# Attention preparation spread over two iterations, and the first two MLP groups prepared in the last batches

## The chip, the cores and the metric

The kernel runs on one core of a Trainium2 chip. The metric is the device time of one execution in microseconds.

## The reference

One transformer block with conditioning, for x of 8 batches x 256 tokens x 144 channels (16 heads of 9):

```
sh1, sc1, g1, sh2, sc2, g2 = split(swish(c) @ w_mod + b_mod, 6)
xn  = ln(x) * (1 + sc1) + sh1
q, k, v = heads(xn @ w_qkv + b_qkv)
q = ln(q) * g_q ; k = ln(k) * g_k            # over the 9 channels of a head
o = softmax(q k^T / 3) v
x = x + g1 * (o @ w_proj + b_proj)
xn2 = ln(x) * (1 + sc2) + sh2
x = x + g2 * (gelu(xn2 @ w1 + b1) @ w2 + b2)  # hidden width 576
```

## The kernel before

A batch n has its 256 tokens in two tiles of 128 partitions (I = 2). Each of the five engines has a queue written out by hand, with semaphores between them; an engine runs its queue strictly in order, so a wait holds all that stands behind it. The order within an iteration is that of the function `iteration` of each engine's block.

**Attention of batch n** is cut into 8 units u. TensorE makes `scores(n, u)` (L1088, four matmuls into two of the four banks of `ps_s`), ScalarE takes the exponential (`exponentials`, L552), and TensorE multiplies with v (`values(n, u)`, L1103, eight matmuls into `ps_o[:, 1]`). `scores(n, u)` waits for exponential u - 2, `values(n, u)` for exponential u. After units 3 and 7 ScalarE copies the sums out (`output`, L559).

**Preparation of batch b** runs beside the attention of the batches before it, in these steps: GpSimd standardises and modulates x (`standardise` L354, `modulate` L372 and L376); VectorE splits it in a high and a low f16 part (`stack`, L712, L715); TensorE transposes (`transpose_x`, L1015), VectorE copies out (`xT_out`, L721); TensorE multiplies (`make_qkv`, L1022); ScalarE squares (`squares`, L516) and copies the raw q, k, v (`raw_out`, L523); VectorE sums (`sums`, L726); ScalarE takes the roots by Ln and Exp (`roots`, L528, L532); VectorE refines them in three Newton steps (L1276 to L1280) and scales k and q (`norm_qk`, L738); GpSimd multiplies q with the gains (`gains`, L383, L389) and places v (`v_slots`, L397); VectorE splits k and q (`split_k` L750, L753; `split_q` L760, L763; the second instruction of each is the low part, `klo` and `qlo`); TensorE transposes (`transpose_k`, `transpose_q`, L1029) and VectorE copies out (`k_out` L770, `q_out` L777).

**Output of batch n**: TensorE transposes the sums (`transpose_o`, L1113), VectorE divides (`normalise`, L836, L838), TensorE transposes by token (`transpose_o_tok`, L1122), VectorE copies (`channels`, L844), TensorE projects (`project`, L1131), VectorE gates and adds and takes statistics (`projected` L849, `residual` L855, L858).

In iteration n of before, the x of n+2 goes up to qkv, the q and k of n+1 are made, and of n-1 the output is transposed, divided and copied; its projection is in n+1.

**MLP**: four groups k of two batches (T = 4 tiles). VectorE aggregates the statistics (`aggregate`, L928) and standardises (`standardise2`, L901), GpSimd modulates (`modulate2`, L464, L468), VectorE splits (`stack2`, L912, L915), TensorE transposes (`transpose_z`, L1197), VectorE copies out (`zT_out`, L922), TensorE makes 5 hidden tiles of a group (`hidden`, L1209), ScalarE takes gelu (L609), TensorE multiplies with w2 (`mlp_out`, L1226), VectorE finishes (`final`, L943, L949). The weights w1 are split by one GpSimd instruction (L446) and one of VectorE (L964). Before, all of group 0 to 2 gets its roots at once, after the residual of batch 5, and `transpose_z(0)` stands in TensorE's queue behind the last batch's seventh unit.

Of the kernel before, what the change touches and what calls it, by code (L numbers as in the profile page):

```python
# [90 lines left out]
def build(nc, x, cT, w_mod, b_mod, w_qkv, g_q, g_k, w_proj, b_proj, w1, w2, b2, ident, lo_rows, out):  # L91
    with ExitStack() as ctx:
# [80 lines left out]
        T = 2 * I  # L173
        EARLY = (NB - 1) * T
# [96 lines left out]
        def proj_bank(n):  # L271

            return ps_o[:, 0, :] if n < B - 2 else ps_x[:, 1, :]

# [57 lines left out]
        def _(pool):  # L332
# [105 lines left out]
            for it in range(1, 2):  # L438
                iteration(it * 2, 0)
                iteration(it * 2 + 1, 1)  # L440
            iteration(B - 4, 0)
            iteration(B - 3, 1, norms=False)
            iteration(B - 2, 0, norms=False)
# [38 lines left out]
        def _(act):  # L482
# [79 lines left out]
            def early_roots():  # L562

                act.wait_ge(stat2, EARLY)
                nc.scalar.activation(ly2[:, 0:EARLY], mv2[:, 0:EARLY, 1], ACT.Ln, bias=eps[:, 0:1]).then_inc(root_act.sem, 1)
                act.wait_ge(root_act.sem, root_act.after(0, "ln"))
                nc.scalar.activation(y2[:, 0:EARLY], ly2[:, 0:EARLY], ACT.Exp, scale=-0.5).then_inc(root_act.sem, 1)

            def iteration(n, par, first=False, makes=True, ahead=True):
# [21 lines left out]
                exponentials(n, 6)  # L591
# [3 lines left out]
            for it in range((B - 4) // 2):  # L595
                iteration(it * 2 + 1, 1)
# [5 lines left out]
            output(B - 1, 1, 1)  # L602
# [11 lines left out]
        def _(dve):  # L614
# [245 lines left out]
            def iteration(n, par, first=False, makes=True, ahead=True):  # L860

                if ahead and not first:
                    stack(n + 2, prep)
                if makes:
                    sums(n + 1, prep)
                if ahead and first:
                    stack(n + 2, prep)
                if n >= 2:
                    projected(n - 2)
                if makes:  # L870
                    norm_qk(n + 1, prep)
                if not first:
                    normalise(n - 1)
                if makes:
                    split_k(n + 1, prep)
                if not first:
                    channels(n - 1)
# [6 lines left out]
                if n >= 2:  # L884
                    residual(n - 2)
# [447 lines left out]
```

## Time and profile before

| | us |
|---|---|
| median of 3 runs (lowest, highest) | 204.68 (202.39, 205.91) |
| the profiled execution | 202.29 |
| its span in the trace | 200.5 |
| TensorE busy | 166.0 (83%) |
| VectorE busy | 125.7 (63%) |
| ScalarE busy | 108.9 (54%) |
| GpSimd busy | 65.5 (33%) |

The span is the time from the first to the last instruction of the trace. A busy time is the union of the engine's instructions; two that follow each other on an engine overlap a little, so the time that one takes in a queue (start to next start) is a little less than its duration. "Clock" is the share of TensorE's full clock that was granted: 1.00 is 2.4 GHz, 0.50 is 1.2 GHz.

### The profile page before, as it was taken

What the parts mean: (1) busy time and instruction counts of PE and PEld (TensorE: products, weight loads), DVE (VectorE), ACT (ScalarE), POOL (GpSimd) and SP (SyncE); (2) the same over time, 40 slices, a digit from 0 to 9 for tenths busy, and PEclk for the clock granted to TensorE, in tenths of its full rate; (3) what the DMA queues carried; (4) which work ended last, traced back from release to release, by engine and by line L of the source; (5) the groups of instructions that cost most, each with busy time, mean ns of one, the idle gap of its engine ahead of it and who ended that gap; (6) DMA issues with size and microseconds to landing.
All of it is one profiled execution on the core that took longest, in us unless ns stands there. A gap on an engine that the chain in (4) does not pass through costs nothing.

```text
span 200.5 us, 3873 instructions
## 1 busy us (share of the span) xinstructions
PE 166.0 (83%) x1504; PEld 93.9 (47%) x1504; DVE 125.7 (63%) x312; ACT 108.9 (54%) x146; POOL 65.5 (33%) x81
## 2 busy tenths in 40 slices
PE   0009982749979999999999999899659999999983
PEld 0005131413434454544644545344316796979773
DVE  3269568819548587679677774955856786564212
ACT  2001024255998879978888799976842404132320
POOL 8103513067418146173290201600462352220000
PEclk9999999999999999999999999999856999999999
DMA  0993028950000000000000000000000000101101
GB/s 10 247 211 120 5 51 251 399 158 0 3 2 0 3 3 0 0 3 0 3 0 5 0 3 2 0 3 0 3 0 0 0 3 0 60 3 59 59 0 59
DMA packets 4535, 8.67 MB, mean 43 GB/s; under 512 B 821, under 2 KB 3071, under 8 KB 4406
## 3 DMA queue, kind: packets, MB, share of 16 engines
q1 hardware_dynamic: 4228, 8.41, 14.0%
q8 instruction: 12, 0.20, 0.4%
q14 instruction: 7, 0.06, 0.1%
q10 hardware_dynamic: 288, 0.01, 0.1%
HBM read 7.21 MB, written 1.21 MB: 42 GB/s over the span
## 4 chain that ended last, share of the span: by engine, by line
PE 73%; DVE 9%; DMA 6%; ACT 3%; POOL 3%; issue 3%; SPq 1%; POOLq 0%; ACTq 0%
PE ps_o L1103 15%; PE ps_o L1226 10%; PE ps_s L1209 9%; PE ps_s L1088 8%; PE ps_x L1022 8%; DMA pTs<-in_b_mod 6%; PE ps_x L1029 4%; PE ps_o L1131 4%; PE ps_x L1113 4%; PE ps_s L1006 3%; PE ps_o L1015 3%; PE ps_x L1197 2%; PE ps_s L1000 2%; POOL z2s L464 2%; DVE kst L753 2%
## 5 line engine op out<-in xcount | busy, mean ns | idle before, releaser
L552 ACT ACTIVATE pTs<-ps_s,escale 128x1024 f32<-128x1024 f32 x64 | 68.9, 1109 | 17.1 <-PE ps_s L1088 16.1
L1103 PE MATMUL ps_o<-pTs,v 128*32 128x256 f32 x512 | 42.9, 410 | 5.0 <-ACT raw L523 2.5
L609 ACT ACTIVATE late<-ps_s 120x512 f32<-120x512 f32 (+1 forms) x20 | 11.9, 596 | 26.1 <-PE ps_s L1209 26.1
L1088 PE MATMUL ps_s<-qT,kT 32*128 32x256 f16 x256 | 24.3, 282 | 1.0 <-DVE qT L777 1.0
L1226 PE MATMUL ps_o<-w_sb,late 120*128 120x144 f32 (+1 forms) x160 | 20.7, 287 | 0.7 <-ACT late L609 0.7
L1226 PEld LDWEIGHTS ps_o<-w_sb,late 120*128 120x128 f32 (+1 forms) x160 | 19.9, 190 | 1.2 <-ACT late L609 1.2
L1209 PE MATMUL ps_s<-late,w1s 110*120 110x512 f16 (+1 forms) x80 | 18.8, 386 | 0.0
L1103 PEld LDWEIGHTS ps_o<-pTs,v 128*32 128x32 f32 x512 | 10.5, 110 | 17.5 <-ACT pTs L552 7.1
L1088 PEld LDWEIGHTS ps_s<-qT,kT 32*128 32x128 f16 x256 | 7.1, 93 | 24.4 <-issue 20.8
L464 POOL TENSOR_TENSOR z2s<-z2s,mbc 128x576 f32<-128x576 f32 x4 | 8.4, 2092 | 28.7 <-DVE z2s L901 28.7
L397 POOL COPY v<-raw 128x288 f32<-128x288 f32 x8 | 4.0, 496 | 41.8 <-DVE ssum L726 34.9
L1000 PE MATMUL ps_s<-pTs,c_s 73*128 73x288 f32 (+1 forms) x8 | 4.2, 707 | 15.1 <-DMA pTs<-in_b_mod 15.1
L1022 PE MATMUL ps_x<-wq,xT 110*128 110x432 f16 x64 | 15.9, 401 | 0.8 <-DVE xT L721 0.8
L354 POOL TENSOR_SCALAR z<-xall,mv,rstd 128x144 f32<-128x144 f32 x14 | 13.2, 951 | 10.2 <-DVE rstd L1280 5.2
L726 DVE TENSOR_REDUCE ssum<-sq 128x64 f32<-128x576 f32 x8 | 6.0, 752 | 13.8 <-ACT sq L516 13.8
L1209 PEld LDWEIGHTS ps_s<-late,w1s 110*120 110x120 f16 (+1 forms) x80 | 10.5, 134 | 6.8 <-issue 1.2
L559 ACT ACTIVATE oT<-ps_o 128x512 f32<-128x512 f32 x16 | 9.6, 599 | 3.9 <-PE ps_o L1103 3.9
L389 POOL TENSOR_TENSOR qg<-qn,gbc 128x288 f32<-128x288 f32 x8 | 6.7, 832 | 14.7 <-DVE qn L738 14.7
L943 DVE TENSOR_TENSOR late<-ps_o,mbc 128x288 f32<-128x288 f32 x8 | 3.6, 454 | 11.5 <-PE ps_o L1226 11.5
L1022 PEld LDWEIGHTS ps_x<-wq,xT 110*128 110x128 f16 x64 | 6.3, 108 | 9.4 <-issue 5.4
L1000 PEld LDWEIGHTS ps_s<-pTs,c_s 73*128 73x128 f32 (+1 forms) x8 | 2.5, 330 | 16.0 <-DMA pTs<-in_b_mod 15.1
L1113 PE MATMUL ps_x<-id,oT 128*128 128x128 f32 x64 | 8.7, 278 | 1.2 <-ACT oT L559 1.2
(115 smaller groups left out, 263.4 us busy)
## 6 DMA issues: line engine op xcount, KB each, us to landing
mbc<-mod_rows SPq DMA_DIRECT2D x6, 432.0 KB, 7.4
late<-in_w SPq DMA_DIRECT2D x1, 990.0 KB
xall<-in_x SPq DMA_DIRECT2D x1, 864.0 KB, 13.6
out<-late SPq DMA_DIRECT2D x3, 288.0 KB, 2.3
z2s<-in_w_qkv SPq DMA_DIRECT2D x1, 742.5 KB
mbc<-mod_rows SPq DMA_DIRECT2D x2, 288.0 KB, 6.4
pTs<-in_w_mod SPq DMA_DIRECT2D x1, 486.0 KB
w_sb<-in_w SPq DMA_DIRECT2D x1, 337.5 KB
```

Source lines behind the costliest of these rows:

```text
L354: nc.gpsimd.tensor_scalar(z[:, i, :], xall[:, b, i * H:(i + 1) * H], mv[:, t, 0:1], rstd[:, t:t + 1], ALU.subtract, ALU.mult).then_inc(S.m ...
L464: nc.gpsimd.tensor_tensor(by_batch(z2a), by_batch(z2), m2(k, A2), ALU.mult).then_inc(ln2_mod.sem, 1)
L552: nc.scalar.activation(pT[u % NP].rearrange("p g n -> p (g n)"), ps_s[:, 2 * (u % 2):2 * (u % 2) + 2, :].rearrange("p a n -> p (a n)"), AC ...
L559: nc.scalar.activation(oT[par][:, 2 * pair:2 * pair + 2, :].rearrange("p j n -> p (j n)"), ps_o[:, 1, :], ACT.Copy).then_inc(o_out, 1)
L609: nc.scalar.activation(hT[k % 2][0:FW[f], f, :], ps_s[0:FW[f], (NF * k + f) % 4, :], ACT.Gelu_apprx_tanh, scale=UNSCALE).then_inc(gelued, 1)
L1000: mm = nc.tensor.matmul(ps_s[:, 2 + b, 0:2 * H], c_s[0:k, h, b:b + 1].broadcast_to([k, P]), wm_sb[0:k, h, 0:2 * H], start=(h == 0), stop=( ...
L1022: mm = nc.tensor.matmul(ps_x[:, i, 0:QKV], xT[:, c, i * P:(i + 1) * P], wq[:, c, :], start=(c == 0), stop=(c == NC - 1))
L1088: mm = nc.tensor.matmul(ps_s[:, 2 * (u % 2) + a, half * N:(half + 1) * N], kT[par][rows, j, i * P:(i + 1) * P], qT[par][rows, j, :], start ...
L1103: mm = nc.tensor.matmul(ps_o[SLOT * g:SLOT * (g + 1), 1, (j % 2) * N:(j % 2 + 1) * N], v[par][:, i, h, :], pT[u % NP][:, g, :], start=(i = ...
L1113: tr = nc.tensor.transpose(ot[:, i, j // 2, j % 2], oT[par][:, j, i * P:(i + 1) * P], id32[:])
L1209: mm = nc.tensor.matmul(ps_s[0:FW[f], m % 4, :], w1s[:, c, f * FT:f * FT + FW[f]], zT[k % 2][:, c, :], start=(c == 0), stop=(c == NC - 1))
L1226: mm = nc.tensor.matmul(ps_o[:, n, i * H:(i + 1) * H], hT[k % 2][0:r, f, t * P:(t + 1) * P], w2_sb[0:r, f, :], start=(f == 0), stop=(f == ...
```

## The change

- The preparation of a batch is spread over two iterations: in iteration n the qkv, squares, raw copy, sums and roots are those of n+2 (x of n+3 is stacked and transposed, x of n+4 standardised), while norms, splits and transposes of q and k are those of n+1, made right at the start of the iteration.
- The output is later: `transpose_o` of n-1 stands near the end of iteration n, `normalise(n - 1)` is VectorE's last step of the iteration, and the transpose by token, `channels`, projection and residual of n-1 follow in iteration n+1 (there as n-2).
- The statistics' roots are taken in three parts: the first 8 tiles (groups 0 and 1) in iteration 6 (aggregated ahead of `norm_qk(7)`), the next 4 in batch 7, the last 4 at the end as before.
- z of group 0 is standardised in iteration 6, its transposes lie in batch 7 between the units, in halves and through another bank; z of group 1 follows in batch 7 too. `hidden(0, 0..1)` comes ahead of batch 7's last values.
- GpSimd's w1 product moves ahead of iteration 2, VectorE's w1 split into iteration 6. In the MLP the pieces of group 0 and 1 interleave with the last batch's output.

GpSimd and ScalarE:

```
-            def iteration(n, par, norms=True):
-
-
+            def iteration(n, par):
+
+
+                gains(n + 1, prep)
                 v_slots(n + 1, 1 - par)
-                gains(n + 1, prep)
-                if norms:
-                    standardise(n + 3, prep)
-                    modulate(n + 3, prep)
+                for b in range(n + 4 if n else 3, min(n + 5, B)):
+                    standardise(b, prep)
+                    modulate(b, prep)
 
...
-
             pool.wait_ge(ld_w1, 16)
             nc.gpsimd.tensor_scalar(w1_h, w1_f, WS, lo_row[:, 0:1], ALU.mult, ALU.mult).then_inc(w1_made, 1)
+            for n in range(2, B - 1):
+                iteration(n, n % 2)
...
+            def iteration(n, par, first=False):
 
 
                 exponentials(n, 0)
+                if not first:
+                    output(n - 1, 1, 1 - par)
+                exponentials(n, 1)
                 if first:
-                    exponentials(n, 1)
-                if makes:
                     squares(n + 1, prep)
                     raw_out(n + 1, prep)
-                if not first:
-                    output(n - 1, 1, 1 - par)
-                if makes:
+                exponentials(n, 2)
+                if first:
                     roots(n + 1, prep)
-                if not first:
-                    exponentials(n, 1)
-                exponentials(n, 2)
                 exponentials(n, 3)
-                if not makes:
-                    early_roots()
+                if n == B - 2:
+                    early_roots(0, slice(0, READY))
                 exponentials(n, 4)
                 output(n, 0, par)
                 exponentials(n, 5)
-                exponentials(n, 6)
+                if n == B - 1:
+                    early_roots(1, slice(READY, EARLY))
+                if first:
+                    exponentials(n, 6)
+                if n + 2 < B:
+                    squares(n + 2, prep)
+                    raw_out(n + 2, prep)
+                if not first:
+                    exponentials(n, 6)
+                if n + 2 < B:
+                    roots(n + 2, prep)
                 exponentials(n, 7)
 
             iteration(0, 0, first=True)
-            for it in range((B - 4) // 2):
-                iteration(it * 2 + 1, 1)
-                iteration(it * 2 + 2, 0)
-            iteration(B - 3, 1)
-            iteration(B - 2, 0, ahead=False)
-            iteration(B - 1, 1, makes=False, ahead=False)
+            for n in range(1, B):
+                iteration(n, n % 2)
...
             for k in range(NB):
                 for f in range(NF):
+                    if (k, f) == (0, 2):
+                        output(B - 1, 1, 1)
```

VectorE (the iteration of before is among the functions printed above), and the order after the last iteration:

```
+            def first_half_z():
+
+                roots(0, ready)
+                standardise2(0)
+                dve.wait_ge(w1_made, 1)
+                nc.vector.scalar_tensor_tensor(w1s[:], w1_f, WS, w1_h, ALU.mult, ALU.subtract).then_inc(w1_made, 1)
+
+            def iteration(n, par, first=False):
+
+                if first:
+                    sums(n + 1, prep)
+                    stack(n + 2, prep)
+                if n == B - 2:
+                    aggregate(ready)
+                norm_qk(n + 1, prep)
+                split_k(n + 1, prep)
+                if n >= 2:
+                    channels(n - 2)
+                split_q(n + 1, prep)
+                if first:
+                    xT_out(n + 2, prep)
+                k_out(n + 1, prep, 1 - par)
+                q_out(n + 1, prep, 1 - par)
+                if n == B - 2:
+                    first_half_z()
+                if n + 3 < B:
+                    stack(n + 3, prep)
+                if n >= 2:
+                    projected(n - 2)
+                    residual(n - 2)
+                if n + 2 < B:
+                    sums(n + 2, prep)
+                if n + 3 < B:
+                    xT_out(n + 3, prep)
+                if not first:
+                    normalise(n - 1)
+
...
-            early, late_tiles = range(EARLY), range(EARLY, B * I)
+            channels(B - 3)
+            stack2(0)
+            normalise(B - 2)
             projected(B - 3)
-            normalise(B - 2)
             residual(B - 3)
             aggregate(early)
-            dve.wait_ge(root_act.sem, root_act.after(0, "y0"))
-            roots(0, early)
-            standardise2(0)
             channels(B - 2)
-
-            dve.wait_ge(w1_made, 1)
-            nc.vector.scalar_tensor_tensor(w1s[:], w1_f, WS, w1_h, ALU.mult, ALU.subtract).then_inc(w1_made, 1)
+            zT_half(0, 0)
+            standardise2(1)
+            zT_half(0, 1)
+            dve.wait_ge(w1_made, 2)
+            nc.vector.memset(hT[1][FW[-1]:FW[-1] + 1, NF - 1, :], 1.0).then_inc(h_ones, 1)
+            roots(1, early)
+            stack2(1)
+            zT_half(1, 0)
             projected(B - 2)
-            stack2(0)
             residual(B - 2)
-            zT_out(0)
-            standardise2(1)
+            zT_half(1, 1)
+            standardise2(2)
             normalise(B - 1)
-            stack2(1)
             channels(B - 1)
-            standardise2(2)
+            stack2(2)
             projected(B - 1)
             residual(B - 1)
-            dve.wait_ge(w1_made, 2)
-            nc.vector.memset(hT[1][FW[-1]:FW[-1] + 1, NF - 1, :], 1.0).then_inc(h_ones, 1)
-            zT_out(1)
-            stack2(2)
             aggregate(late_tiles)
             dve.wait_ge(root_pool, 2)
-            roots(1, late_tiles)
+            roots(2, late_tiles)
+            standardise2(3)
```

TensorE (the new iteration alone, then the last batch after the change):

```
            def iteration(n, par):

                values(n - 1, 7, 1 - par)
                scores(n, 1, par)
                if n >= 2:
                    transpose_o_tok(n - 2)
                scores(n, 2, par)
                values(n, 0, par)
                transpose_k(n + 1, prep)
                scores(n, 3, par)
                values(n, 1, par)
                if n >= 2:
                    pe.wait_ge(post_dve.sem, post_dve.after(n - 2, "och"))
                transpose_q(n + 1, prep)
                scores(n, 4, par)
                values(n, 2, par)
                if n + 2 < B:
                    pe.wait_ge(prep.x.sem, prep.x.after(n + 2, "xT"))
                if n >= 2:
                    project(n - 2)
                scores(n, 5, par)
                values(n, 3, par)
                pe.wait_ge(prep.dve.sem, prep.dve.after(n + 1, "qT"))
                if n + 2 < B:
                    make_qkv(n + 2, prep)
                scores(n, 6, par)
                values(n, 4, par)
                if n + 3 < B:
                    if n >= 2:
                        pe.wait_ge(gated, n - 1)
                    transpose_x(n + 3, prep)
                scores(n, 7, par)
                values(n, 5, par)
                if n + 2 < B:
                    qkv_used(n + 2, prep)
                transpose_o(n - 1, 1 - par)
                scores(n + 1, 0, 1 - par)
                values(n, 6, par)
...
+            def transpose_z_half(k, h):
+                pe.wait_ge(ln2_parts.sem, ln2_parts.after(k, "zlo"))
+                if k < 2 and (k or h):
+                    pe.wait_ge(ln2_T.sem, ln2_T.after(k, f"zT{h}") - 1)
+                if k > 2:
+                    pe.wait_ge(ln2_T.sem, ln2_T.after(k - 1, f"zT{h}"))
+                for c in range(2):
+                    for t in range(T):
+                        tr = nc.tensor.transpose(z_bank(k, h)[0:KR, c, t * P:(t + 1) * P],
+                                                 zst[:, t * NC + 2 * h + c, 0:KR], id16[:])
+                tr.then_inc(ln2_pe.sem, 1)
...
            n, par = B - 1, 1
            values(n - 1, 7, 1 - par)
            scores(n, 1, par)
            transpose_o_tok(n - 2)
            scores(n, 2, par)
            values(n, 0, par)
            pe.wait_ge(post_dve.sem, post_dve.after(n - 2, "och"))
            transpose_o(n - 1, 1 - par)
            scores(n, 3, par)
            values(n, 1, par)
            project(n - 2)
            scores(n, 4, par)
            values(n, 2, par)
            transpose_o_tok(n - 1)
            scores(n, 5, par)
            values(n, 3, par)
            pe.wait_ge(gated, n - 1)
            transpose_z_half(0, 0)
            scores(n, 6, par)
            values(n, 4, par)
            project(n - 1)
            scores(n, 7, par)
            values(n, 5, par)
            transpose_z_half(0, 1)
            values(n, 6, par)
            transpose_z_half(1, 0)
            pe.wait_ge(w1_made, 2)
            hidden(0, range(0, 2))
            values(n, 7, par)
            pe.wait_ge(exped, B * U)
            hidden(0, range(2, NF))
            transpose_z_half(1, 1)
            pe.wait_ge(gated, B - 1)
            transpose_o(n, par)
            hidden(1, range(0, 2))
            transpose_o_tok(n)
            pe.wait_ge(o_out, B * 2)
            mlp_out(0, range(0, 1))
            project(n)
            mlp_out(0, range(1, 2))
            hidden(1, range(2, NF))
            pe.wait_ge(gated, B)
            transpose_z(2)
            mlp_out(1)
            for k in range(2, NB):
                hidden(k, range(NF))
                if k + 1 < NB:
                    transpose_z(k + 1)
```

## Rows read from the trace of the kernel before

**Rows 1.** Busy time by stage: length; PE, PEld, DVE, ACT, POOL busy; clock, DMA.

```profile
82.88:96.00 13.12, 13.12 (x150) 6.53 (x152) 10.02 (x22) 11.30 (x15) 5.90 (x7) 1.00 0.01 2
121.61:133.30 11.69, 11.02 (x133) 5.43 (x132) 9.75 (x19) 9.99 (x13) 3.87 (x4) 1.00 0.01 2
133.30:160.80 27.50, 23.06 (x187) 13.28 (x187) 16.91 (x48) 15.13 (x20) 8.54 (x5) 0.81 0.00 1
```

**Rows 2.** Chain that ended last, batch 3 to 4: start, us, what.

```profile
83.20 1.18 PE ps_o L1131 x8
...
84.71 1.02 PE ps_x L1113 x8
...
86.30 0.58 PE ps_o L1015 x8
...
88.34 0.32 PE ps_s L1088 x4
...
88.67 0.56 PE ps_x L1122 x4
...
90.12 0.55 PE ps_x L1029 x8
...
93.87 1.57 PE ps_x L1022 x8
...
95.43 0.57 PE ps_o L1103 x8
```

**Rows 3.** Order of time, first batch's end: start, us, engine, line; idle before.

```profile
56.35 0.65 ACT L516 ACTIVATE sq<-ps_x 128x576 f32<-128x576 f32 x1 [0.30 <-PE ps_x L1022]
...
57.67 0.60 ACT L559 ACTIVATE oT<-ps_o 128x512 f32<-128x512 f32 x1
...
58.70 2.10 ACT L552 ACTIVATE pTs<-ps_s,escale 128x1024 f32<-128x1024 f32 x2
...
58.42 1.06 PE L1113 MATMUL ps_x<-id,oT 128*128 128x128 f32 x8 [1.20 <-ACT oT L559]
```

**Rows 4.** Order of time, VectorE in a middle iteration.

```profile
84.82 0.23 DVE L1276 SCALAR_TENSOR_TENSOR qnt<-qy 128x64 f32<-128x64 f32 x1
...
86.34 0.35 DVE L836 RECIPROCAL rden<-ps_x 128x32 f32<-128x32 f32 x1
...
87.10 0.53 DVE L750 CAST kst<-kn 128x576 f16<-128x576 f32 x1
...
89.27 0.69 DVE L844 COPY o_ch<-ps_x 72x512 f32<-72x512 f32 x1 [1.00 <-PE ps_x L1122]
```

**Rows 5.** Order of time, batch 1's split of k beside GpSimd.

```profile
47.76 0.94 POOL L389 TENSOR_TENSOR qg<-qn,gbc 128x288 f32<-128x288 f32 x1 [1.48 <-DVE qn L738]
48.09 0.93 DVE L753 TENSOR_TENSOR kst<-kn,kst 128x288 f16<-128x288 f32 x1
```

**Rows 6.** Order of time, low parts of q and k, and a standardising GpSimd.

```profile
87.29 1.89 POOL L354 TENSOR_SCALAR z<-xall,mv,rstd 128x144 f32<-128x144 f32 x2
...
87.66 0.60 DVE L753 TENSOR_TENSOR kst<-kn,kst 128x288 f16<-128x288 f32 x1
...
90.36 0.98 DVE L763 TENSOR_TENSOR qst<-qg,qst 128x288 f16<-128x288 f32 x1
...
116.61 0.50 DVE L763 TENSOR_TENSOR qst<-qg,qst 128x288 f16<-128x288 f32 x1
...
127.03 2.33 DVE L753 TENSOR_TENSOR kst<-kn,kst 128x288 f16<-128x288 f32 x1
```

**Rows 7.** Order of time, VectorE aggregates twelve tiles.

```profile
139.56 0.91 DVE L928 BATCH_NORM_AGGREGATE mv<-bst 128x2 f32<-128x6 f32 x12
```

**Rows 8.** Order of time, the last batch and the preparation of z.

```profile
143.58 1.91 PE L1131 MATMUL ps_x<-wp_sb,o_ch 73*128 73x144 f32 x8
...
149.50 0.76 DVE L915 TENSOR_TENSOR zst<-z2s,zst 128x576 f16<-128x576 f32 x1
...
163.07 0.48 DVE L977 MEMSET late<- 1x512 f32 x1 [0.16 <-issue]
```

More of the change, by code:

```diff
@@ L858, in residual @@
                     nc.vector.bn_stats(bst[:, n * I + i, :], xall[:, n, i * H:(i + 1) * H]).then_inc(res_dve.sem, 1)
[L860 to L877, printed above, removed]
-                if makes:
-                    split_q(n + 1, prep)
-                    k_out(n + 1, prep, 1 - par)
-                    q_out(n + 1, prep, 1 - par)
-                if ahead:
-                    xT_out(n + 2, prep)
-                if n >= 2:
-                    residual(n - 2)
-            dve.wait_ge(o_ones, 1)
-            iteration(0, 0, first=True)
-            for it in range((B - 4) // 2):
-                iteration(it * 2 + 1, 1)
-                iteration(it * 2 + 2, 0)
-            iteration(B - 3, 1)
-            iteration(B - 2, 0, ahead=False)
             def standardise2(k):
@@ L930, in roots @@
             def roots(part, tiles):
+                if part < 2:
+                    dve.wait_ge(root_act.sem, root_act.after(part, "y0"))
                 dve.wait_ge(stat2, tiles.stop)
@@ L934, in roots @@
                 dve.wait_ge(root_dve.sem, root_dve.after(part, "rstd"))
+            ready, early, late_tiles = range(READY), range(READY, EARLY), range(EARLY, B * I)
+            def first_half_z():
[31 more added lines that the diff above has]
+                    normalise(n - 1)
+            dve.wait_ge(o_ones, 1)
+            iteration(0, 0, first=True)
+            for n in range(1, B - 1):
+                iteration(n, n % 2)
             def final(k):
@@ L1164, in iteration @@
-                scores(n, 6, par)
-                if makes:
-                    if not first:
-                        pe.wait_ge(post_dve.sem, post_dve.after(n - 1, "och"))
-                    transpose_q(n + 1, prep)
+                    transpose_x(n + 3, prep)
+                scores(n, 7, par)
                 values(n, 5, par)
-                scores(n, 7, par)
-                if makes:
-                    scores(n + 1, 0, 1 - par)
+                if n + 2 < B:
+                    qkv_used(n + 2, prep)
@@ L1182, in _, with transpose_z_half @@
             make_qkv(1, prep)
[L1183 to L1188 removed]
+            for u in (1, 2):
+                scores(0, u, 0)
+            values(0, 0, 0)
+            transpose_x(2, prep)
+            scores(0, 3, 0)
+            values(0, 1, 0)
+            scores(0, 4, 0)
+            values(0, 2, 0)
+            qkv_used(1, prep)
+            transpose_k(1, prep)
+            scores(0, 5, 0)
+            values(0, 3, 0)
+            transpose_q(1, prep)
+            scores(0, 6, 0)
+            values(0, 4, 0)
+            scores(0, 7, 0)
+            values(0, 5, 0)
+            pe.wait_ge(prep.dve.sem, prep.dve.after(1, "qT"))
+            make_qkv(2, prep)
+            scores(1, 0, 1)
+            values(0, 6, 0)
+            transpose_x(3, prep)
+            for n in range(1, B - 1):
+                iteration(n, n % 2)
+            def transpose_z_half(k, h):
+                pe.wait_ge(ln2_parts.sem, ln2_parts.after(k, "zlo"))
+                if k < 2 and (k or h):
+                    pe.wait_ge(ln2_T.sem, ln2_T.after(k, f"zT{h}") - 1)
+                if k > 2:
+                    pe.wait_ge(ln2_T.sem, ln2_T.after(k - 1, f"zT{h}"))
+                for c in range(2):
+                    for t in range(T):
+                        tr = nc.tensor.transpose(z_bank(k, h)[0:KR, c, t * P:(t + 1) * P],
+                                                 zst[:, t * NC + 2 * h + c, 0:KR], id16[:])
+                tr.then_inc(ln2_pe.sem, 1)
             def transpose_z(k):
[L1191 removed]
                 for h in range(2):
[L1193 to L1199 removed]
+                    transpose_z_half(k, h)
             def hidden(k, tiles):
```

128 lines of the change are left out of this document (51 added, 77 removed).

## Prediction

> **What bounds the kernel now.** I read the busy time by stage first, then the chain that ended last, then the order of time engine by engine. In a middle iteration the tensor engine is busy for the whole of its 13.12 us at full clock [rows 1], and the chain consists of its pieces alone. The pieces of one iteration are eight score groups of 0.32, eight value groups of 0.57, both head transposes at 0.55, transpose of x 0.58, qkv 1.57, projection 1.18, transposes of o 1.02 and of o by token 0.56 [rows 2]: 2.56 + 4.56 + 1.10 + 0.58 + 1.57 + 1.18 + 1.02 + 0.56 = 13.13. So no reordering gains anything there; it can only open waits. What can be gained lies around the last batches. From 121.61 to 133.30 TensorE idles 0.67 us. From 133.30 to 160.80 it idles 27.50 - 23.06 = 4.44 us, and the mean clock is 0.81: 2 x 0.19 x 27.50 = 10.4 us at the lower level (1.2 GHz), of which some 2.3 us are idle; the other 8.1 us of work would take half as long at 2.4 GHz, so the low clock costs about 4.05 us. Together 8.5 us is all that z made early can win. From 161 us on the MLP keeps the tensor engine full, and the change leaves it so.
>
> **The change part by part.** The number of instructions is the same but for one more root of the residual statistics; TensorE's work is the same. So I count what idle and slow time each stage has after.
>
> *Start (batches 0 and 1).* Queue order on ScalarE is now exponential 6, squares and raw of batch 2, roots of batch 2, exponential 7. Before, exponential 7 ran ahead of them. The squares start at 56.35, 0.1 us after qkv has ended, and the exponential behind the roots starts at 58.70, with one output copy in between that is no longer there (57.67 to the next start, 0.5) [rows 3]: 58.70 - 56.35 - 0.5 + 0.1 = 1.95, and exponential 7 takes 1.11 more with the hand-over. Until 3.1 us after qkv values 7 of batch 0 can't start; TensorE has score 0, values 6 and the transpose of x(3) for it, 0.32 + 0.57 + 0.58 = 1.47 [rows 2]. Wait: 1.6 to 1.7 us, and about 0.3 more behind it, because exponential 0 and the output copy follow in the same queue. In exchange the present wait of 1.2 us ahead of the transposes of o(0) [rows 3] goes (those now come late, when raw has long been out), and values 0 of batch 0, now ahead of the first wait, saves little since the work is at the cold pace. Net **+1.0 us**.
>
> *Middle iterations, n = 2 to 5.* This is the part I weigh most. VectorE's queue now has normalise(n-2) as the last act of iteration n-1 and norm_qk, split_k, channels, split_q as the first of iteration n. All of it hangs behind the transposes of o, which TensorE issues near the end of n-1, and two transposes wait for it: k for klo and q for qlo. From the start of the transposes of o: 1.09 + 0.04 until the denominators start; normalise 87.10 - 86.34 = 0.77; norm_qk 86.34 - 84.82 = 1.52 [rows 4]; the high part of k 0.5. The low part of k took 0.93 in the first batches, where it came right behind qn and so beside GpSimd's product qg; those rows have exactly the new order [rows 5]. klo ends at 1.13 + 0.77 + 1.52 + 0.50 + 0.93 = 4.85. TensorE has by then done o 1.02, score 0, values 6, values 7, score 1, o by token, score 2, values 0 = 1.02 + 3 x 0.32 + 3 x 0.57 + 0.56 = 4.25 [rows 2]. Wait 0.6. Then q: channels 0.61 (busy 0.69, the next instruction starts 0.08 before its end), high part of q 0.55, low part 0.60: qlo ends at 4.77 + 0.61 + 0.55 + 0.60 = 6.53. TensorE comes there after k 0.55, score 3 and values 1: 4.25 + 1.44 = 5.69. So in all 6.57 - 5.69 = 0.9 us per iteration. Since the next transposes of o lie behind this wait, it comes back each time: 4 x 0.9 = **+3.6 us**. Bounds: with the low parts undisturbed (0.50 at 116.61 [rows 6]) qlo ends at 5.9, wait 0.2; with the low part of q stretched as at 90.36 (0.98 [rows 6]), wait 1.3. I take 0.9, since GpSimd will standardise beside it, as it did beside the middle value, 0.60 at 87.66 [rows 6]. ScalarE has 11.3 us of work in an iteration and by the new order ends exponential 7 about 0.15 us before TensorE wants it, so it adds nothing while the above wait stands.
>
> The Trainium skill, page SBUF — State Buffer, section Who interferes with whom, says that VectorE and GpSimd share a port pair by an exclusive lock and that the loser blocks for the whole instruction. The trace agrees at 127.03, where the low part of k took 2.33 us beside GpSimd's long w1 product. By that rule qlo could have to wait for a whole standardising instruction (1.89 us for two [rows 6]), up to 0.95 us: a wait of 1.7 instead of 0.9.
>
> *Iteration 6.* The same chain, but aggregate(8 tiles) now stands ahead of norm_qk: 12 took 0.91 [rows 7], so 0.6; GpSimd has no batch to standardise, so qlo takes 0.50: wait 0.9 + 0.6 - 0.2 = 1.3. With no qkv left, values 4 and score 7 run into the output copy and exponential 5 behind it: values 3 end, 0.11, copy 0.5, exponential 1.11, against score 6 and values 4 of 0.89: another 0.86. 2.2 - 0.67 present idle = **+1.5 us**. GpSimd's w1 product moves from here to before iteration 2. It stretched klo to 2.33 [rows 6]; there it meets the stacking and sums of batches 3 and 4, which have over 2 us of slack before their users, so it costs nothing; without that cover up to 1.9.
>
> *Last batch and group 1.* roots(0), standardise2(0) and the w1 split lie in iteration 6 behind q_out; nobody waits for them but projected(4), residual(4) and normalise(5), the last of which is ready when the transposes of o(5) are. z(0) is complete some 4 us before its transposes. The waits for och(n-2), gated and output copies are met. The one new wait is the first half of z(1): its zlo is queued on VectorE behind zT_half(0,1), which waits for TensorE's own transposes behind score 7. From the start of that half transpose: 0.45 (half of 16 transposes, an estimate from 0.55 for eight over 128 rows) + 0.1, copy 0.61 (as channels), memset 0.5 [rows 8], three Newton steps 0.6 (0.23 each for more elements [rows 4]), two stacking instructions 0.8 + 0.76 [rows 8] = 3.8, against 0.45 + 0.57 of TensorE work: **idle 2.8 us**. In the present end, with its 4.44 us of idle, the projection at 143.58 took 1.91 us [rows 8] against 1.18 [rows 2], at the lower level. So I expect a fall here too, but behind one idle instead of several: less than half of the present 8.1 us of slow work, I take 3.6, cost **1.8**. After that hidden(0), hidden(1) and both outputs follow without a gap. This stage: 2.8 + 1.8 - 8.5 = **-3.9 us**.
>
> Sum: 1.0 + 3.6 + 1.5 - 3.9 = +2.2 us.
>
> **Rivals.** (A) The VectorE chain is not disturbed by GpSimd and the clock holds through the 2.8 us idle: middle 4 x 0.2 = 0.8, iteration 6 +0.9, end -5.7: 1.0 + 0.8 + 0.9 - 5.7 = -3.0, 201.7. For it: klo took 0.60 in the middle iterations; against it: qg starts 0.17 after the high part in this very order. (B) Slower: the low part of q loses to whole GpSimd instructions, each middle wait becomes 1.7: 4 x 0.8 = 3.2 more, total +5.4, 210.1. It decides as soon as qlo waits over 0.4 us more than at 87 us; the row with 0.98 speaks for it. The shared port rule of the Trainium skill's SBUF page is what would bring it. (C) The early z isn't early or the waits don't arise: TensorE stays as full in the last batches as its work allows, neither the 2.8 us nor the middle waits arise: 1.0 + 0 + 0.2 - 8.5 = -7, 197.7. Against it: the queue orders above force both. (D) The idle brings the low clock back for long, as before (8.1 us of work at half pace): cost 4.05 instead of 1.8, +4.5, 209.2.
>
> **How the numbers follow.** The profiled execution took 202.29 (span 200.5 and 1.8 around it) and is the fastest of the runs shown; the median is 204.68. 2.2 us on that median is 206.9. Chances: forecast 0.42; A 0.20; B 0.15; C 0.09; D 0.14. 2% is 4.1 us, about what a measurement here can tell from no change. Faster by over 2% is C and a sliver of A: 0.10. Slower is B, D and the upper edge of the forecast: 0.29. The rest, 0.61, within. Range: from A less 1 us to B plus 1 us, 200.5 to 211.5; the forecast's own is 204.5 to 209.
>
> **What would show it.** Idle of TensorE ahead of the k and q transposes released by klo and qlo, 0.9 us in each of iterations 2 to 5; an iteration of 14.0 us; an idle of 1.7 us ahead of the first batch's last values; an idle of 2.8 us ahead of the transposes of z(1) and a clock below 1 behind it, and nowhere else. The prediction is wrong if the middle iterations stay at 13.1 us, if klo takes 0.5, if ScalarE becomes what TensorE waits for, or if more than some 4 us run at the low clock.

## The result, and the profile after

| | before | after |
|---|---|---|
| median of all runs, us | 203.73 (4 runs) | 207.38 (4 runs) |
| lowest to highest | 202.39 to 205.91 | 206.19 to 208.03 |
| profiled execution | 202.29 | 207.80 |
| its span | 200.5 | 206.0 |

The ratio of after to before is 1.0166, 95% interval 1.0114 to 1.0218: slower by 1 to 2%. The two profiled executions differ by 5.5 us, more than the medians (3.65), as before's lies below all four of its runs and after's is the second slowest of its four. The places below are the profiled executions' own and add up to their 5.5. Ratios leave out the slow runs of a kernel (one of 276.5 us in experiment 1 among them), and where many of its runs are slow the median of all of them stands beside the ratio.

Busy time by stage of before, then of after, each with its own cuts: score 0 of batch 0, the first values group of iterations 2, 6 and 7, the output of the first MLP group, the end (length; PE, PEld, DVE, ACT, POOL busy; clock; DMA):

```profile
38.40:69.10 30.70, 26.57 (x272) 11.13 (x272) 18.04 (x47) 23.70 (x30) 14.75 (x18) 1.00 0.15 47
69.10:121.60 52.50, 52.50 (x593) 26.12 (x592) 38.62 (x86) 45.20 (x56) 19.20 (x24) 1.00 0.01 2
121.60:133.60 12.00, 11.04 (x133) 5.43 (x132) 9.75 (x19) 10.29 (x14) 3.87 (x4) 1.00 0.01 2
133.60:160.80 27.20, 23.06 (x186) 13.28 (x187) 16.91 (x48) 14.83 (x20) 8.54 (x5) 0.81 0.00 1
160.80:200.50 39.70, 35.73 (x269) 30.13 (x267) 18.18 (x42) 8.94 (x15) 6.82 (x6) 1.00 0.09 31
```

```profile
38.40:71.90 33.50, 28.37 (x280) 11.88 (x284) 19.23 (x48) 24.61 (x34) 19.88 (x24) 0.90 0.14 44
71.90:127.60 55.70, 52.11 (x592) 25.63 (x584) 40.10 (x93) 44.70 (x57) 15.56 (x20) 1.00 0.01 2
127.60:140.30 12.70, 11.24 (x136) 5.56 (x140) 12.14 (x29) 10.11 (x13) 6.42 (x4) 1.00 0.01 1
140.30:167.90 27.60, 24.51 (x209) 13.69 (x202) 14.83 (x39) 15.25 (x21) 4.29 (x4) 0.88 0.00 1
167.90:206.00 38.10, 34.18 (x254) 29.23 (x252) 18.19 (x40) 8.02 (x14) 5.77 (x6) 1.00 0.09 32
```

The start took 2.8 us more, iterations 2 to 5 took 3.2 more, iteration 6 took 0.7 more, and the two last stages together 65.7 instead of 66.9, 1.2 less: 2.8 + 3.2 + 0.7 - 1.2 = 5.5. In the middle TensorE was busy for the whole of before's stage and idles 3.6 us in after's. The work of the stages isn't quite the same: iteration 5 of after has no x left to transpose (0.58 us less), and batch 7 has the transposes of o(5) by token (0.56 more).

One middle iteration of after in order of time, rows of VectorE, GpSimd and TensorE:

```profile
84.04 1.09 PE L1128 MATMUL ps_x<-id,oT 128*128 128x128 f32 x8
...
85.17 0.36 DVE L840 RECIPROCAL rden<-ps_x 128x32 f32<-128x32 f32 x1 [1.23 <-PE ps_x L1128]
...
87.61 0.94 POOL L394 TENSOR_TENSOR qg<-qn,gbc 128x288 f32<-128x288 f32 x1 [7.01 <-DVE qn L742]
87.93 0.94 DVE L757 TENSOR_TENSOR kst<-kn,kst 128x288 f16<-128x288 f32 x1
...
88.93 0.62 PE L1044 MATMUL ps_x<-id,kst 128*128 128x128 f16 x8 [0.70 <-DVE kst L757]
...
89.87 0.64 DVE L767 TENSOR_TENSOR qst<-qg,qst 128x288 f16<-128x288 f32 x1
...
90.62 0.61 PE L1044 MATMUL ps_x<-id,qst 128*128 128x128 f16 x8 [0.18 <-issue]
...
103.90 0.51 DVE L767 TENSOR_TENSOR qst<-qg,qst 128x288 f16<-128x288 f32 x1
```

Read it as a chain: transposes of o from 84.04, denominators at 85.17, klo from 87.93 to 88.87, and only then the transposes of k, 0.70 us late; the transposes of q come 0.18 later than TensorE could. The next transposes of o begin at 98.06, 14.02 us after these; before it was 13.12 [rows 1]. In iterations 4 and 5 no batch is left for GpSimd to standardise: qlo (the last row) takes 0.51 instead of 0.64, nothing is waited for ahead of q, and the transposes of k come 13.88 and 13.83 us apart. VectorE itself waits 1.23 us for the transposes of o, though the sums of the next batch have been taken by then: that is the place to repair.

The end, TensorE of after, to be read against [rows 8]:

```profile
152.21 0.64 PE L1118 MATMUL ps_o<-pTs,v 128*32 128x256 f32 x8
155.89 1.10 PE L1228 MATMUL ps_o<-id,zst 128*110 128x128 f16 x8 [3.04 <-DVE zst L884]
156.78 3.62 PE L1246 MATMUL ps_s<-late,w1s 110*120 110x512 f16 x8
160.33 1.08 PE L1118 MATMUL ps_o<-pTs,v 128*32 128x256 f32 x8
161.34 3.02 PE L1246 MATMUL ps_s<-late,w1s 110*120 110x512 f16 x12
164.20 0.61 PE L1228 MATMUL ps_o<-id,zst 128*110 128x128 f16 x8
```

An idle of 3.04 us for the low part of z(1), and then eight hidden matmuls in 3.62 us and values in 1.08 instead of 0.64: the lower level. By the stage's clock 2 x 0.12 x 27.6 = 6.6 us passed at it, 0.9 of them still idle. What it cost is read from start to start: the half transpose took 0.89 us where the next one took 0.45, eight hidden matmuls 3.55 (1.81 from 165.60 on), values 1.01 (0.57), twelve hidden matmuls 2.86 (2.59 from 173.78 on), together 2.9 us more.

The start, TensorE of after, where values groups ran at 1.08 until 52.6 us (values 0, ahead of the idle of 2.89, had taken 0.64 at 42.45):

```profile
45.98 1.10 PE L1030 MATMUL ps_o<-id,xst 128*110 128x128 f16 x8 [2.89 <-DVE xst L719]
...
51.61 1.08 PE L1118 MATMUL ps_o<-pTs,v 128*32 128x256 f32 x8
52.63 0.62 PE L1044 MATMUL ps_x<-id,qst 128*128 128x128 f16 x8
...
60.14 0.64 PE L1118 MATMUL ps_o<-pTs,v 128*32 128x256 f32 x8 [1.73 <-ACT pTs L552]
```

### The profile page after: what moved, and what is told of

Same layout as the page of the kernel before. It is cut to its first block, busy times and chain, and to the rows that moved or that the text cites. A ratio compares the mean times of both kernels' runs of the same rounds, so it can differ in the third digit from the quotient of the medians.

```text
span 206.0 us, 3890 instructions
## 1 busy us (share of the span) xinstructions
PE 167.5 (81%) x1504; PEld 93.9 (46%) x1504; DVE 128.8 (63%) x315; ACT 108.6 (53%) x148; POOL 64.2 (31%) x81
## 4 chain that ended last, share of the span: by engine, by line
PE 69%; DVE 15%; DMA 6%; issue 4%; ACT 4%; SPq 1%; ACTq 0%; DVEq 0%
PE ps_o L1118 12%; PE ps_o L1263 10%; PE ps_s L1246 9%; PE ps_x L1037 8%; PE ps_s L1103 7%; DMA pTs<-in_b_mod 6%; PE ps_x L1044 4%; PE ps_x L1128 4%; PE ps_o L1146 3%; PE ps_s L1021 3%; DVE kst L757 3%; PE ps_o L1030 2%; PE ps_s L1015 2%; ACT pTs L552 2%; DVE o_tok L842 1%
## 5 line engine op out<-in xcount | busy, mean ns | idle before, releaser
L1118 PE MATMUL ps_o<-pTs,v 128*32 128x256 f32 x512 | 41.6, 405 | 2.7 <-ACT pTs L552 2.1
L1103 PE MATMUL ps_s<-qT,kT 32*128 32x256 f16 x256 | 25.7, 284 | 1.6 <-DVE qT L781 1.0
L394 POOL TENSOR_TENSOR qg<-qn,gbc 128x288 f32<-128x288 f32 x8 | 7.5, 942 | 46.6 <-DVE qn L742 46.6
L1246 PE MATMUL ps_s<-late,w1s 110*120 110x512 f16 (+1 forms) x80 | 20.3, 408 | 0.0
L464 POOL TENSOR_TENSOR z2s<-z2s,mbc 128x576 f32<-128x576 f32 x4 | 7.8, 1954 | 29.5 <-DVE z2s L870 29.5
L359 POOL TENSOR_SCALAR z<-xall,mv,rstd 128x144 f32<-128x144 f32 x14 | 13.7, 989 | 10.3 <-DVE rstd L1325 5.2
L1246 PEld LDWEIGHTS ps_s<-late,w1s 110*120 110x120 f16 (+1 forms) x80 | 11.0, 142 | 7.5 <-issue 2.2
L1030 PE MATMUL ps_o<-id,xst 128*110 128x128 f16 x64 | 6.6, 260 | 5.4 <-DVE xst L719 5.4
L1044 PE MATMUL ps_x<-id,kst 128*128 128x128 f16 x64 | 5.8, 243 | 5.4 <-DVE kst L757 5.4
L1030 PEld LDWEIGHTS ps_o<-id,xst 128*110 128x110 f16 x64 | 5.2, 159 | 10.1 <-DVE xst L719 6.6
```

The costliest lines, as they stand in the source:

```text
L359: nc.gpsimd.tensor_scalar(z[:, i, :], xall[:, b, i * H:(i + 1) * H], mv[:, t, 0:1], rstd[:, t:t + 1], ALU.subtract, ALU.mult).then_inc(S.m ...
L1030: tr = nc.tensor.transpose(bank[0:KR, c, i * P:(i + 1) * P], xst[:, i * NC + c, 0:KR], id16[:])
L1044: tr = nc.tensor.transpose(bank16(bank)[:, j, i * P:(i + 1) * P], st[:, i * NH + 4 * j:i * NH + 4 * j + 4, :].rearrange("p h s -> p (h s)" ...
L1103: mm = nc.tensor.matmul(ps_s[:, 2 * (u % 2) + a, half * N:(half + 1) * N], kT[par][rows, j, i * P:(i + 1) * P], qT[par][rows, j, :], start ...
L1118: mm = nc.tensor.matmul(ps_o[SLOT * g:SLOT * (g + 1), 1, (j % 2) * N:(j % 2 + 1) * N], v[par][:, i, h, :], pT[u % NP][:, g, :], start=(i = ...
L1246: mm = nc.tensor.matmul(ps_s[0:FW[f], m % 4, :], w1s[:, c, f * FT:f * FT + FW[f]], zT[k % 2][:, c, :], start=(c == 0), stop=(c == NC - 1))
```

## The experiments

Each is one change to the changed kernel unless said otherwise. `iteration` means the function of the engine named.

**1. Norms of the next batch ahead of normalise.** ScalarE takes the roots of n+2 ahead of exponential 6, VectorE does norm_qk(n+2) at the end of iteration n.

```diff
 # ScalarE
                     raw_out(n + 2, prep)
+                    roots(n + 2, prep)
                 if not first:
                     exponentials(n, 6)
-                if n + 2 < B:
-                    roots(n + 2, prep)
 # VectorE
-                norm_qk(n + 1, prep)
+                if first:
+                    norm_qk(n + 1, prep)
...
                     xT_out(n + 3, prep)
+                if n + 2 < B:
+                    norm_qk(n + 2, prep)
                 if not first:
                     normalise(n - 1)
```

> The changed kernel with the roots of batch n+2 taken ahead of exponential 6 and norm_qk(n+2) placed ahead of normalise(n-1), in VectorE's idle time before the transposes of o end (1.23 us in the changed kernel). Theory (the chain transposes of o, normalise, norm_qk, split_k holds the tensor engine): the wait of 0.70 us for klo goes and the iteration falls from 14.02 us to 13.1 to 13.3; four iterations and the sixth save 3 to 4 us, span about 202.5, ratio to the kernel before about 1.00. Rival (ScalarE has become the bound, 0.15 us of slack behind exponential 7): roots ahead of exponential 6 push exponentials 6 and 7 back 0.65 us, the tensor engine waits for them instead and the iteration stays at 13.7 us or more.

Measured: ratio 0.9992 (0.9945 to 1.0039), span 202.3, 3.7 us under that of the changed kernel. The median of all ten runs is 203.06. TensorE's waits for klo are gone from iterations 2 to 6. Two qkv groups, 13.14 us apart, in TensorE's order of time:

```profile
79.27 1.63 PE L1039 MATMUL ps_x<-wq,xT 110*128 110x432 f16 x8
...
92.41 1.63 PE L1039 MATMUL ps_x<-wq,xT 110*128 110x432 f16 x8
```

The theory holds: VectorE's chain behind the transposes of o set the iteration. ScalarE did not become the bound in the middle; a wait of 0.48 us for an exponential appears only once, at 123.63, where the changed kernel has one of 0.35 at 127.58.

**2. Exponential 7 first, in the first batch.**

```diff
                 if first:
                     exponentials(n, 6)
+                    exponentials(n, 7)
...
-                exponentials(n, 7)
+                if not first:
+                    exponentials(n, 7)
```

> The changed kernel, but in the first batch exponential 7 runs ahead of the squares, raw copy and roots of batch 2. Theory of the prediction (the first batch loses 1.7 us because exponential 7 is queued behind the roots): the idle of 1.73 us goes, 1.4 to 2 us saved. Rival (the next thing is late as well: klo of batch 2 hangs on the same roots and comes 2.9 us after them): the idle only moves to the transposes of k(2), the time changes by under 0.4 us.

Measured: ratio 1.0133 (1.0001 to 1.0266), median of all 208.57 (4 runs). TensorE in order of time:

```profile
60.37 0.39 PE L1105 MATMUL ps_s<-qT,kT 32*128 32x256 f16 x4 [0.83 <-ACT pTs L552]
60.94 0.64 PE L1120 MATMUL ps_o<-pTs,v 128*32 128x256 f32 x8 [0.18 <-ACT oT L559]
62.35 0.62 PE L1046 MATMUL ps_x<-id,kst 128*128 128x128 f16 x8 [0.77 <-DVE kst L759]
```

The idle of 1.73 ahead of values 7 is now 0.83 ahead of score 2 and 0.77 ahead of the transposes of k(2), which begin at 62.35; in the changed kernel they begin at 62.30. The three waits here add up to 1.78 us, the two of the changed kernel in this place (1.73 and 0.18) to 1.91. The rival holds for the idle: what sets this place is the way from qkv(2) over the roots to klo(2), and the queue order of exponential 7 costs next to nothing. The times can't show it, as four runs lie 4 us apart and in the profiled one the low pace came back at 63.4 us.

**3. The first half of z(1) later in TensorE's queue.**

```diff
             values(n, 6, par)
-            transpose_z_half(1, 0)
             pe.wait_ge(w1_made, 2)
             hidden(0, range(0, 2))
             values(n, 7, par)
+            transpose_z_half(1, 0)
             pe.wait_ge(exped, B * U)
```

> The changed kernel, but the first half transpose of z(1) stands behind hidden(0, 0..1) and values 7 in the tensor engine's queue. Theory (the idle of 3.04 us for zlo of z(1) brings the low clock): the idle falls to about 0.3 us before hidden and up to 0.6 us before the half transpose, no low clock behind it (stage clock 1.00 against 0.87), 2.2 us of idle and 3.3 us of slow work saved, 5.5 us in all. Rival (the low clock comes anyway, from the looser last batches): only the idle is saved, 2.2 us, and some 6 us of the stage still run at the low level.

Measured: ratio 0.9977 (0.9933 to 1.0021), span 201.9. The stretch from late in iteration 6 to the MLP, and the two places where TensorE still waits:

```profile
138.40:166.50 28.10, 27.21 (x258) 16.79 (x259) 19.41 (x48) 18.19 (x24) 8.86 (x6) 1.00 0.01 2
```

```profile
154.28 1.91 PE L1246 MATMUL ps_s<-late,w1s 110*120 110x512 f16 x8 [0.26 <-issue]
...
157.06 0.65 PE L1228 MATMUL ps_o<-id,zst 128*110 128x128 f16 x8 [0.30 <-DVE zst L884]
```

The idle fell from 3.04 to 0.56 us and the clock of the stretch is 1.00. The median over all runs fell from 207.38 to 202.79, 4.6 us, and the span by 4.1. From the transposes of k(7) to the end it is 5.3 us less (131.83 to 201.9 against 130.66 to 206.0; this execution lost 1.2 us ahead of them): 2.5 of idle and 2.8 of slow work, which fits the 2.9 read from the rows above, not the 3.3 expected. The rival, that the low clock comes anyway, is out: in all five profiles with the idle of 3.04 us (the changed kernel and experiments 1, 2, 4 and 5) the low level followed, in none of the three with this repair (3, 6 and 7).

**4. GpSimd's gains behind klo.** One execution.

```diff
-                pool.wait_ge(S.dve.sem, S.dve.after(b, "qn"))
+                pool.wait_ge(S.dve.sem, S.dve.after(b, "klo" if S is prep else "qn"))
```

> The changed kernel, but GpSimd's product qg waits for klo, so that VectorE's low part of k has no GpSimd instruction beside it. Theory (klo takes 0.94 us because qg runs beside it and both read memory through what they share): klo takes 0.46 in the middle iterations and the idle before the transposes of k falls from 0.70 to about 0.2; qg starts 0.9 us later and the wait moves on to q, 1 us or more there. Rival (klo is slow in this place for its own reasons, for example right behind its own high part): klo stays at 0.9.

Measured: span 210.0. All eight klo of this kernel and, below, of the changed one (duration min/median/max):

```profile
L757 DVE TENSOR_TENSOR kst<-kn,kst x8: 460/461/463, 34.8 to 134.7; 128x288 f16<-128x288 f32 x8
```

```profile
L757 DVE TENSOR_TENSOR kst<-kn,kst x8: 928/936/943, 34.5 to 129.7; 128x288 f16<-128x288 f32 x8
```

klo takes 461 ns without qg beside it and 936 ns with it. The idle ahead of k fell to 0.22 and that ahead of q rose to 0.80 in iterations 2 and 3 and to 0.66 behind them (1 us or more was expected): the theory holds, and the contention itself can't be avoided by waiting, as q needs qg. Of the 4.0 us that the span is longer, 3.9 lie ahead of iteration 2's transposes of k, where the low pace lasted longer and came back (values at 1.08 from 63.4 to 69 us). The Trainium skill, page SBUF — State Buffer, section Who interferes with whom, says that a VectorE instruction with two inputs in SBUF contends with a reading GpSimd instruction by an exclusive lock. For klo and qg the trace agrees: qg takes 0.80 alone (in this experiment) and klo 0.46, and in the changed kernel both together take those 1.26 us, from qg's start at 87.61 to klo's end at 88.87, as if one ran behind the other. For qlo it does not bear out a wait for a whole instruction: beside a GpSimd standardising instruction, which reads SBUF too, qlo took 0.64 instead of 0.51.

**5. Values 0 of batch 0 in its old place.**

```diff
-            values(0, 0, 0)
             transpose_x(2, prep)
+            values(0, 0, 0)
             scores(0, 3, 0)
```

> The changed kernel, but values 0 of batch 0 stand behind the transposes of x(2) as in the kernel before. In the changed kernel the tensor engine runs at the low pace until 52.6 us, in the kernel before until 48.2. Theory (the early values 0 bring an idle of 2.9 us behind them and so the second stretch at the low level): with the old order low pace ends near 48 us, 1.5 to 2 us saved. Rival (the length of the low stretch doesn't hang on this order but on work that is too thin behind it: ScalarE and VectorE are awaited until 53 us): the low pace ends after 52 us again, nothing saved.

Measured: ratio 1.0156 (1.0013 to 1.0299), median of all 208.63 (4 runs). In the profiled execution the idle ahead of the transposes of x(2) was 3.45 us and values still took 1.08 at 53.12. The place of values 0 is not what lengthened the low stretch.

**6. Both repairs** (1 and 3).

> The changed kernel with both repairs: norm_qk of the next batch ahead of normalise (first experiment) and the first half transpose of z(1) behind hidden(0, 0..1) and values 7 (third). Theory (the two losses are independent): 3.7 and 4 to 5 us off the changed kernel, ratio to the kernel before 0.975 to 0.985. Rival (fuller middle batches bring nothing since the last batches then wait for z(0)): ratio 0.99 or more.

Measured: ratio 0.9799 (0.973 to 0.9869), median 199.80 of 6 runs against 204.55, span 198.2. The two losses are independent: 206.0 - 198.2 = 7.8 us against 3.7 + 4.1 one by one.

**7. As 6, with x(2) stacked ahead of the sums of batch 1.**

```diff
                 if first:
-                    sums(n + 1, prep)
                     stack(n + 2, prep)
+                    sums(n + 1, prep)
```

> As the kernel with both repairs, but in the first batch VectorE stacks x(2) ahead of the sums of batch 1, as soon as GpSimd has it. Theory (the idle before the transposes of x(2), 2.9 us, decides how long the low pace lasts): the idle falls to 2.2 us and the low pace ends before 51 us instead of 52.6, 1 us saved against the kernel with both repairs. Rival (it varies from run to run whatever the idle): no difference beyond the 0.3 us of the order itself.

Measured: ratio 0.9796 (0.9704 to 0.9888), as without it. The idle was 2.23 us, the shortest of these kernels, and yet in the profiled execution this stretch ran wholly at the lower level, which lasted until 59.7 us:

```profile
46.00:58.00 12.00, 11.49 (x87) 4.10 (x86) 7.18 (x15) 5.81 (x8) 8.67 (x11) 0.50 0.01 1
```

The length of that idle alone does not decide how long the low pace lasts. It varied from profile to profile: it ended at 51.8 us in experiment 3, 52.6 in the changed kernel, 54 in experiment 5.

**8. The early z alone.** The iterations of all engines are those of the kernel before; z of groups 0 and 1, the roots in three parts and the place of the w1 product are those of the change, with repair 3. Its core on VectorE:

```diff
             def iteration(n, par, first=False):
...
+                ahead = n + 2 < B
                 if n == B - 2:
                     aggregate(ready)
-                norm_qk(n + 1, prep)
-                split_k(n + 1, prep)
-                if n >= 2:
-                    channels(n - 2)
...
+                if ahead and not first:
+                    stack(n + 2, prep)
+                sums(n + 1, prep)
...
+                if n >= 2:
+                    projected(n - 2)
+                norm_qk(n + 1, prep)
+                if not first:
+                    normalise(n - 1)
+                split_k(n + 1, prep)
+                if not first:
+                    channels(n - 1)
+                split_q(n + 1, prep)
...
                 if n == B - 2:
                     first_half_z()
```

> One part of the change alone: the iterations are those of the kernel before (preparation of n+1 and n+2, output of n-1), while z of groups 0 and 1 is made early as in the changed kernel, with the w1 product ahead of iteration 2 and the first half transpose of z(1) behind values 7. Theory (the gain lies in the early z alone, and the spreading of preparation and output costs the start and the middle iterations): iterations stay at 13.12 us, the idle of 4.4 us and the 8.1 us of slow work in the last batches go, 6 to 8.5 us off the kernel before, ratio 0.96 to 0.97. Rival (without the looser output of n-2 VectorE can't fit z(0) and z(1) in the last batches): the tensor engine waits 3 us or more there, ratio 0.985 or more.

Measured: ratio 0.9706 (0.9606 to 0.9806), but the median of all seven is 203.48: two ran in 197.02 and 198.65 with a mean clock of 0.998 and 0.989, one in 201.31 with 0.998, so that the mean clock doesn't account for all of the spread, and four in 203.48 to 205.29 with 0.958 to 0.975. The profiled one is of the latter; TensorE in order of time:

```profile
143.61 1.07 PE L1129 MATMUL ps_x<-id,o_tok 128*72 128x128 f32 x4 [2.55 <-DVE o_tok L837]
144.61 0.61 PE L1095 MATMUL ps_s<-qT,kT 32*128 32x256 f16 x4
145.15 1.08 PE L1110 MATMUL ps_o<-pTs,v 128*32 128x256 f32 x8
```

VectorE stacked z(0) first, for which it waited for GpSimd, and normalise(6) came behind it; TensorE idled 2.55 us and the pace halved.

**9. The same, normalise(6) first.**

```diff
             projected(B - 3)
+            normalise(B - 2)
             residual(B - 3)
-            aggregate(early)
             stack2(0)
-            normalise(B - 2)
             channels(B - 2)
+            aggregate(early)
```

The aggregation moves behind channels(6) with it.

> The early z alone, as in the experiment before, but on VectorE normalise(6) stands directly behind projected(5), ahead of the stacking of z(0) that waits for GpSimd. Theory (what held the early z alone back is the idle of 2.55 us before the transposes of o(6) by token, and the low clock that follows it in most runs: 204 us with it, 197.0 without it): idle under 0.5 us, clock of the stage 1.00 in nearly all runs, time 194 to 197 us, ratio 0.95 to 0.965. Rival (the low clock in the last batches comes from the thinner work there, whatever this one wait): the times stay in two clusters, ratio about 0.97 or more.

Measured: ratio 0.971 (0.9646 to 0.9774), median 196.47 of 6 runs (195.28 to 197.68) against 203.24 of before, span 194.8. That is the upper end of the time expected; the ratio, expected as 0.95 to 0.965, is a little above (by the medians 0.967). One cluster of times, and in the profiled execution full clock to the end; two of the six had a mean clock of 0.972 and took 197.6. Stages by busy time:

```profile
69.00:121.00 52.00, 52.00 (x591) 25.89 (x590) 38.69 (x87) 44.70 (x57) 19.20 (x24) 1.00 0.01 2
121.00:134.00 13.00, 12.32 (x143) 6.05 (x145) 9.36 (x33) 11.86 (x17) 1.50 (x3) 1.00 0.01 2
134.00:160.00 26.00, 24.39 (x227) 15.44 (x220) 20.24 (x45) 15.74 (x21) 10.97 (x6) 1.00 0.00 1
```

A single wait in the last batches is over 0.4 us (1.05 at 142.13, for z(0), where under 0.5 was expected). Of the change, the early z is the part that pays; the spreading of preparation and output over two iterations isn't needed for it, against the rival.

## Why the prediction was right, and where not

The forecast was a little slower, 206.9 us; it was 207.4. The two are closer than the forecast deserves: it stood on a median of 204.68 of three runs, and over four runs before's median was 203.73, so the medians moved by +3.65 and not by the +2.2 forecast. Between profiled executions there were +5.5. By the steps of the prediction:

- **No gain in the middle, only waits; 0.9 us for each iteration.** Right in mechanism, and for iterations 2 and 3 in size: 14.02 us against 13.12, the wait for klo 0.70 with 0.6 forecast, klo 0.94 with 0.93. Shown by experiments 1 (the wait goes when the chain is moved) and 4 (the half that is contention). That qlo would be the later of the two by 0.3 was 0.18 there and nothing in iterations 4 and 5, where GpSimd has no batch left to standardise; the forecast counted 0.9 four times. (Its own terms give 6.53 - 5.69 = 0.84.) That the stage still came to +3.2 with 3.6 forecast is in part chance: a wait of 0.35 us for an exponential, just ahead of iteration 6, and one transpose of x less both fall into it. The rival that q loses a whole GpSimd instruction did not come: qlo took 0.64.
- **Start, +1.0 us.** The idle grew by the 1.0 forecast: 33.5 - 28.37 = 5.1 us against 30.7 - 26.57 = 4.1. The sum fits by luck. The forecast's terms give 1.65 + 0.3 - 1.2 = 0.75, and measured they give 1.73 + 0.18 - 1.20 = 0.7; the rest is the first wait, 2.89 us against 2.51, which the forecast had at no cost. The reason given, exponential 7 behind the roots, is not what sets the place either: experiment 2 took that order away, and the transposes of k(2) began at 62.35 instead of 62.30. The term that failed is the pace: TensorE's busy time in this stage rose by 1.8 us for almost the same work, above all since values still ran at 1.08 us at 51.6 instead of turning fast at about 48. I had left the start's clock unpriced. Experiments 5 and 7 excluded two causes in the order there. That the change brings this loss isn't shown: with the start's order of before the low pace ended at 48.2 us in before's profile, at 49.8 in experiment 9's and at 54.0 in experiment 8's. What decides the length of this stretch stays open, and part of the 5.5 us between two profiled executions can be chance.
- **Iteration 6, +1.5 us.** It was +0.7, or about +1.1 with the wait of 0.35 us just ahead of its cut. The wait for klo was 0.67 there, no more than elsewhere, though the aggregation of eight tiles took 0.55 in VectorE's queue (127.14 to 127.69; 0.6 forecast): in the trace TensorE is held itself at 127.58, by the 0.35 for the exponential, and so comes to k later too. No run tried it. The wait at the output copy and exponential 5 was 0.49 + 0.28 with 0.86 forecast.
- **End, -3.9 us.** The idle was 3.04 with 2.8 forecast, for the reason given. The low clock behind it cost 2.9 us instead of 1.8, midway to rival D's 4.05: this size was the weakest term. Before's own low stretch, priced at 4.05, comes to 3.6 when it is read from start to start as above, so there was less to win. From the first values of iteration 7 to the end the idle fell by 1.1 us (8.1 to 7.0), the cost of the low clock by 0.7, and the transposes of o(5) by token came in with 0.56: 1.2 less, as measured. Of before's 4.44 us of idle, 0.36 lies ahead of the cut used here.
- **The signs.** The forecast had called itself wrong if more than some 4 us ran at the low clock. By this sign it was: 6.6 us passed at it in the end, and about 6.7 more in the start (46 to 52.6), where "nowhere else" had been said. The other signs (klo, the 14.0 us, ScalarE in the middle iterations) came out for it.
- **Rival C, that early z wins all it can.** It needed the waits not to arise. (Its sum is 1.0 + 0.2 - 8.5 = -7.3, not -7.) Experiments 6 and 9 made that kernel: 4.8 and 6.8 us under the medians of before beside them.

## What to carry to other kernels

Where one engine is busy all the time, a new order of its queue can only open waits; count the time of the other engine's chain from the step that releases it to the step that waits for it, and put what doesn't depend on that release ahead of it (here the norms ahead of the division). Split a compound change by what each part can win: the early preparation of the MLP brought 3% (experiment 9), and with the spreading beside it nothing was left of that (experiment 3, ratio 0.998), or 2% with the norms ahead of the division (experiment 6). In a tuned tail look first for the one wait that is long, as the clock behind it can cost as much again as the idle itself (here 2.9 us behind 3.04).

## What the hardware showed

- A wait of 2.55 us in the last batches (experiment 8) was followed by the low clock in the profiled execution, and the runs of that kernel fell in groups up to 8 us apart; with waits of up to 1.05 us (experiment 9) all six ran within 2.4 us. In the kernel before, the low level began at 144.0 us, 1.3 us after a wait of 1.73 us.
- In the start the pace halves or not in ways that no order tried here settles. Behind one and the same wait of 1.7 us, ending at 60 to 63 us, values ran on at 0.64 in the changed kernel and experiments 1 and 5, and in experiments 3, 4, 6 and 7 they turned to 1.08 within 4 us. In experiment 2's profile values ran at 0.64 from 53.7 to 61 us and at 1.08 again from 63.4, without any wait over 0.83 us in between.
- The clock column shows 1.00 ahead of the first change of level although the durations there are those of the lower one (values 1.08 us at 45 us in the kernel before); in a start the durations are to be read, not the column.
